# A graph layer on one core: the own side computed from 128 nodes in fp32, and nine batches of rows fetched row by row by ScalarE and SyncE instead of three by ScalarE

## The chip, the core and the metric

The kernel runs on one core of a Trainium2 chip. The metric is the device time of one launch in microseconds: before the change 3934.06 us, median of three runs (3931.01 to 3935.81).

## What is computed

```python
theta = x[dst] - x[src]                       # 412,500 edges, 128 features, fp32
w = sigmoid(relu(theta @ W1 + b1) @ W2 + b2)
agg = segment_sum(w * theta, dst)             # 12,500 nodes; the edges are sorted by dst
indeg = segment_sum(1, dst)
out = layernorm(x + agg + indeg * (x @ W4 + b4))
```

Since theta @ W1 is x[dst] @ W1 - x[src] @ W1, the kernel first projects every node (u = x @ W1) and keeps u and x side by side in a table in HBM, 256 fp32 values (1 KB) a node. For each edge it then needs the row of its source (u for the weight, x for the sum), which is random, and the projection of its destination, the *own side*, which is near in number for neighbouring edges.

## The kernel before, in words

**Tiling.** The edges are cut into 112 chunks of at most 28 tiles of 128 edges; a chunk touches at most 128 neighbouring destination nodes, its window. A chunk is four batches of seven tiles (896 edges), called j = 0 to 3; with a short tail batch there are 449, numbered g.

**Where the rows of the sources come from.** 425 batches are *ringed*: GpSimd gathers them with one indirect DMA a tile (`windows_gpsimd`, L783), into six slots in turn; it may start batch n once batch n-6 has been scaled (`scaled`) and the own side of batch n-2 is there (`z_ready`). 21 batches are *held*: their x rows were gathered at the start (L768), and PE projects them in steps between the other batches. Three batches are fetched *by hand*: ScalarE loads the seven source numbers of one row of tiles into registers (L891) and issues seven DMAs of 1 KB, one for each tile (L895), 128 rows for a batch, one row with each batch g from 40 on. All three share one buffer, since nearly all of the held rows are still in use when it is filled.

**The own side.** x of the window arrives transposed (`winT`) and PE multiplies it with W1 and W4 (`project_window`, L820); DVE adds the biases (`take_window`, L1038 and L1040), which gives `own`, the projections of the window's 128 nodes, and `lin`. `own` in fp32 is then split into three bf16 numbers for each value: ScalarE rounds it (`high`, L910), DVE takes the rest (`take_high`, L1044), ScalarE rounds that (`mid`, L914), DVE takes the last part (`low`, L1048). SyncE stores the three parts to HBM (L672) and loads, for each batch, the 126 rows of 42 nodes from which that batch's own side comes (L666), since a batch touches at most 42 nodes. PE then multiplies these 126 rows with a one-hot matrix in bf16 (L794), whose column for an edge has three ones.

**The rest of a batch.** ScalarE makes the one-hot matrix in two steps (`distance` L875, `one_hot` L883), three batches ahead. DVE subtracts the gathered u (L998), applies relu and the weights W2 (L1004), makes the other one-hot matrix (L1017) and sums to logits (L1012); ScalarE takes the sigmoid (`gate`, L902 and L904); DVE scales x (L1027); PE adds the batch up by node (`add_up`, L812, fp32). In batch j = 1 of a chunk DVE takes the sums of the chunk before (L1033) and finishes its rows (L1060 to L1068), and in j = 2 it normalises them (L971 to L1076).

**Order.** Each engine works through a list written out by hand, in order. SyncE's loop (`windows_sync`) does this for chunk c: `store_parts(c + 1)`, in the middle of which the window of chunk c + 2 is loaded (`load_window`, L690 and L691, after `rows_done`), and then `store_result(c - 1)` (L699), which waits for the normalised rows, that is until batch j = 2 of chunk c. PE's `project_window(c + 2)` stands in chunk c at j = 2 and DVE's `take_window(c + 2)` in chunk c at j = 3.

Of the kernel before, what the change touches and what calls it, by code (L numbers as in the profile page):

```python
# [4 lines left out]
FP32 = mybir.dt.float32  # L5
# [6 lines left out]
P = 128  # L12
# [4 lines left out]
ROUND = 12582912.0  # L17

# [8 lines left out]
NEAR = 42  # L27
WK = 3 * NEAR
# [6 lines left out]
SLOTS = 4  # L35
# [9 lines left out]
HAND = 3  # L45
HAND_FROM = 40
EARLY = 3
# [22 lines left out]
class Sizes:  # L70

    def __init__(self, nodes, edges):
# [28 lines left out]
        self.hand = [HAND_FROM + (P + 2) * (m + 1) + m for m in range(HAND)]  # L101
        assert self.hand[-1] < self.batches and HAND_FROM > self.held[1] and not set(self.hand) & set(self.held)
# [28 lines left out]
def build(nc, x, src, dst, W1, b1, W2, b2, W4, b4, x_cols, x_turned, held_src, src_rows, dst_rows_in, firsts, out):  # L131
    z = Sizes(x.shape[0], src.shape[0])
    with ExitStack() as ctx:
# [15 lines left out]
        near_of = nc.dram_tensor("near_of", (z.rows, NB), FP32, kind="Internal").ap()  # L149
        parts_of = nc.dram_tensor("parts_of", (SLOTS, 3 * P, F), BF16, kind="Internal").ap()  # L150

# [11 lines left out]
        part_no = sb("part_no", [P, 1])  # L163
        node_no = sb("node_no", [P, 1])
# [6 lines left out]
        near_all = sb("near_all", [P, z.rows * NB])  # L171
        near_row = sb("near_row", [P, z.rows * NB], I32)
        neg_ids = sb("neg_ids", [P, z.rows * NB])
# [12 lines left out]
        near_lin = sb("near_lin", [P, NB])  # L186
        last_lin = sb("last_lin", [P, NB])
        held_ends = sb("held_ends", [P, 2])
        none = sb("none", [P, P], I32)
        beyond = sb("beyond", [P, 3, P], I32)  # L190
        extremes = sb("extremes", [P, 10])
        loop_gaps = sb("loop_gaps", [P, PIECES])
        wrong = sb("wrong", [P, 12])
# [8 lines left out]
        parts = sb("parts", [P, 2 * NB, F], BF16)  # L202
        away = sb("away", [P, 2, BATCH], BF16)
        hot_ne = sb("hot_ne", [P, 2, BATCH], BF16)
# [9 lines left out]
        own = sb("own", [P, F])  # L214
        rest = sb("rest", [P, F])
        stage = sb("stage", [P, 2, 3, F], BF16)
# [39 lines left out]
        hand_x = slots_of_x[:, 0:2 * BT * F].rearrange("p (t f) -> p t f", f=2 * F)  # L256
# [57 lines left out]
        const_chain = sem("const_chain")  # L314
# [8 lines left out]
        near_lin_ready = sem("near_lin_ready")  # L323
        near_of_out = sem("near_of_out")
        near_in = sem("near_in")
        near_ready = sem("near_ready")
# [19 lines left out]
        high_ready = sem("high_ready")  # L346
        rest_ready = sem("rest_ready")
        mid_ready = sem("mid_ready")
        low_ready = sem("low_ready")
        parts_out = sems("parts_out", 2)  # L350
        parts_in = sems("parts_in", 2 * NB)
# [67 lines left out]
        def near_no(g):  # L419
            r, j = row_and_place(g)  # L420
            return r * NB + j

# [25 lines left out]
        def hand_row(g):  # L448
            for m, at in enumerate(z.hand):
                row = g - (z.hand[m - 1] + 2 if m else HAND_FROM)  # L450
                if g < at:
                    return (m, row) if 0 <= row < P else None
            return None
# [32 lines left out]
        def place_rows(dve):  # L486
# [20 lines left out]
            for n in range(PIECES):  # L507
# [21 lines left out]
            v.tensor_scalar(held_ends[held_rows, :], row_dst[held_rows, 0:2 * (BATCH - 1):BATCH - 1],  # L529
                            row_base[held_rows, :], None, ALU.subtract)  # L530
# [7 lines left out]
            for bit in range(BITS):  # L538
# [9 lines left out]
            firsts_of = work[0:R, 0:CHUNK].rearrange("p (j e) -> p j e", e=BATCH)  # L548
            v.tensor_scalar(last_lin[0:R, 0:NB - 1], firsts_of[:, 0:NB - 1, BATCH - 1], row_gap[0:R, :], None, ALU.add)
            link(v.tensor_scalar(near_lin[0:R, :], firsts_of[:, :, 0], row_gap[0:R, :], 0.0, ALU.add, ALU.max))  # L550
            link(v.tensor_scalar(near_lin[0:R, :], near_lin[0:R, :], float(P - NEAR), None, ALU.min))
            v.tensor_copy(last_lin[held_rows, 0:1], held_ends[held_rows, 1:2])
            v.tensor_scalar(near_lin[held_rows, 0:1], held_ends[held_rows, 0:1], 0.0, float(P - NEAR), ALU.max, ALU.min)\
                .then_inc(near_lin_ready, 1)
            dve.wait_ge(near_lin_ready, 1)

            for n, at in enumerate((0, P, CHUNK - P)):
                v.tensor_scalar(end_at[0:R, n:n + 1], row_end[0:R, :], float(at), None, ALU.subtract)
            link(v.tensor_copy(last_lin[0:R, NB - 1:NB], extremes[0:R, 5:6]))
# [24 lines left out]

        def place_near(dve):
            v = nc.vector
            dve.wait_ge(near_in, 16)
            v.tensor_scalar(near_row[:, :], near_all[:, :], 3.0, None, ALU.mult).then_inc(near_ready, 1)
            v.tensor_scalar(neg_ids[:, :], near_all[:, :], node_no[:, :], -1.0, ALU.add, ALU.mult)\
                .then_inc(near_ready, 1)  # L590

# [72 lines left out]
        def load_parts(sp, g, row):  # L664
            buf = g % (2 * NB)
            sp.dma_start(parts[0:WK, buf, :], parts_of[chunk_of(g) % SLOTS, bass.ds(row, WK), :])\  # L666
                .then_inc(parts_in[buf], 16)

        def store_parts(sp, c):
            sp.wait_ge(low_ready, c + 1)  # L670
            sp.sem_inc(sp_gate, 1)
            sp.dma_start(parts_of[c % SLOTS, :, :].rearrange("(p m) f -> p m f", m=3), stage[:, c % 2, :, :])\  # L672
                .then_inc(parts_out[c % 2], 16)
            if 0 < c < last_chunk:
                wait(sp, rows_done, c - 1)
                sp.wait_ge(win_ready, c)
                sp.sem_inc(sp_gate, 1)
                load_window(sp, c + 1)
            sp.wait_ge(parts_out[c % 2], 16 * (c // 2 + 1))
            sp.sem_inc(sp_gate, 1)  # L680
            lo, hi = c * NB, end_of(c)
            rows = clamped(near_row, near_no(lo), near_no(lo) + NB, 3 * (P - NEAR))
            if c == last_chunk:
                rows = rows + clamped(near_row, near_no(z.batches), near_no(z.batches) + 1, 3 * (P - NEAR))
            for g in range(lo, hi):
                load_parts(sp, g, rows[g - lo])

# [5 lines left out]
        def store_result(sp, c):  # L693
            sp.wait_ge(y_ready, c + 1)
            if c:
                sp.wait_ge(y_out[(c - 1) % 2], 16 * ((c - 1) // 2 + 1))
            sp.sem_inc(sp_gate, 1)
            base = clamped(base_i, c, c + 1, z.last_base)[0]
            sp.dma_start(out[bass.ds(base, P), :], yout[:, c % 2, :]).then_inc(y_out[c % 2], 16)  # L699

        def windows_sync(sp):
# [22 lines left out]
            for k in range(z.groups):  # L724
# [5 lines left out]
            sp.wait_ge(near_lin_ready, 1)  # L730
            sp.sem_inc(sp_gate, 1)
            sp.dma_start(near_of, near_lin[0:z.rows, :]).then_inc(near_of_out, 16)
            sp.wait_ge(near_of_out, 16)
            sp.sem_inc(sp_gate, 1)
            sp.dma_start(near_all[:, :], near_of.rearrange("(a r) j -> a (r j)", a=1).to_broadcast([P, z.rows * NB]))\
                .then_inc(near_in, 16)
# [680 lines left out]
```

## Time and profile before

| | |
|---|---|
| time, median of 3 runs | 3934.06 us |
| profiled execution: its own time, its span | 3929.44 us, 3927.6 us |
| DVE busy, POOL busy | 2979.7 us (76%), 2953.8 us (75%) |
| PE busy, weight loads | 2018.4 us (51%), 1781.0 us (45%) |
| ScalarE busy | 1255.4 us (32%) |
| mean granted TensorE clock | 0.619 |
| DMA engines | 147 GB/s, about half busy |

Busy shares leave out what an engine's sequencer does by itself: register loads, waits and the issue of DMAs. SyncE does nothing else and so has no busy time at all, and part of ScalarE's list is of this kind. "issue" in a chain or a wait is time in which an engine waited for nothing that the profile shows.

### The profile page before, as it was taken

The page shows a single profiled execution, that of the slowest core. Times are in us where ns is not written, and L with a number is a line of the kernel's source. Part 1 is how long each engine was busy: PE and PEld are TensorE (multiplying, and loading weights), DVE is VectorE, ACT ScalarE, POOL GpSimd, SP SyncE. Part 2 cuts the span into 40 slices and gives each one's busy share as a digit, 9 for nine tenths or more (in the row PEclk, how much of TensorE's full clock was granted, in tenths as well). Part 3 has the DMA queues.
Part 4 walks back from the last instruction along what each step waited for, and adds up shares of the span by engine and source line. Part 5 has one row for each costly group of instructions (what it writes and reads, how often), then busy time and mean ns, then how long its engine had stood idle before and what let it go on. Part 6 is the DMA issues. An engine that isn't in the chain of part 4 may idle for free.

```text
span 3927.6 us, 48444 instructions
## 1 busy us (share of the span) xinstructions
PE 2018.4 (51%) x10531; PEld 1781.0 (45%) x10531; DVE 2979.7 (76%) x4855; ACT 1255.4 (32%) x2220; POOL 2953.8 (75%) x3123
## 2 busy tenths in 40 slices
PE   3245555555545555555555555555555555555554
PEld 2244444444444444444444444444444444444444
DVE  7568777777777777777777777778778777777777
ACT  1223333333333333333333333333333333333332
POOL 7777777777777777777777777777777777777776
PEclk5565665566666556665666656666666665665666
DMA  7445455555555555555555545555555555555553
GB/s 234 131 138 148 144 147 143 146 147 147 147 147 147 147 147 148 146 148 147 147 147 143 148 145 147 147 146 148 148 146 147 147 148 145 146 148 144 149 147 105
DMA packets 343028, 577.99 MB, mean 147 GB/s; under 512 B 127642, under 2 KB 216768, under 8 KB 342501
## 3 DMA queue, kind: packets, MB, share of 16 engines
q0 software_dynamic: 147264, 399.12, 36.0%
q10 hardware_dynamic: 49501, 110.40, 8.7%
q1 hardware_dynamic: 145970, 65.36, 6.2%
q8 instruction: 87, 1.43, 0.1%
q14 instruction: 206, 1.69, 0.1%
HBM read 549.00 MB, written 31.99 MB: 148 GB/s over the span
## 4 chain that ended last, share of the span: by engine, by line
POOL 60%; issue 24%; DVE 8%; ACTq 4%; ACT 2%; DMA 1%; PE 0%; POOLq 0%; DVEq 0%
POOL arena L783 56%; POOL held_x L768 4%; ACTq L895 3%; DVE logit L1012 2%; DVE diff L1004 2%; DVE ps_both L998 1%; DMA arena<-table,lists 1%; ACT away L875 1%; ACTq L891 1%; DVE edge_rows L1027 1%; DVE edge_rows L1017 1%; ACT hot_ne L883 0%; ACT ps_log L902 0%; DVE square L976 0%; DVE rstd L978 0%
## 5 line engine op out<-in xcount | busy, mean ns | idle before, releaser
L783 POOL DMA_INDIRECT arena<-table,lists x2970 | 2810.2, 946 | 905.0 <-issue 899.5
L875 ACT ACTIVATE away<-dst_rows,neg_ids 126x896 bf16<-126x896 bf16 (+1 forms) x449 | 466.4, 1039 | 1587.6 <-issue 1587.6
L812 PE MATMUL ps_win<-edge_rows 128*128 128x130 f32 x3140 | 716.3, 416 | 424.7 <-DVE edge_rows L1027 406.7
L812 PE MATMUL ps_sum<-edge_rows 128*128 128x130 f32 x3136 | 713.4, 415 | 422.2 <-DVE edge_rows L1027 404.3
L812 PEld LDWEIGHTS ps_win<-edge_rows 128*128 128x128 f32 x3140 | 663.2, 319 | 482.8 <-issue 482.6
L812 PEld LDWEIGHTS ps_sum<-edge_rows 128*128 128x128 f32 x3136 | 660.1, 318 | 480.2 <-issue 479.6
L998 DVE TENSOR_TENSOR ps_both<-ps_both,arena 128x896 f32<-128x896 f32 x425 | 467.0, 1099 | 485.6 <-DMA arena<-table,lists 482.0
L794 PE MATMUL ps_both<-parts,hot_ne 126*128 126x128 bf16 x3138 | 334.3, 266 | 958.7 <-ACT hot_ne L883 633.7
L794 PEld LDWEIGHTS ps_both<-parts,hot_ne 126*128 126x128 bf16 x3138 | 245.9, 118 | 1072.1 <-issue 569.7
L1027 DVE TENSOR_TENSOR edge_rows<-arena,ps_log 128x896 f32<-128x896 f32 x425 | 461.5, 1086 | 129.2 <-ACT ps_log L902 129.0
L1004 DVE SCALAR_TENSOR_TENSOR diff<-ps_both,w_rows 128x896 f32<-128x896 f32 (+1 forms) x449 | 489.4, 1090 | 15.4
L1017 DVE TENSOR_TENSOR edge_rows<-ps_log,lists 128x896 f32<-128x896 f32 (+1 forms) x449 | 484.8, 1080 | 0.0
L1012 DVE TENSOR_REDUCE logit<-diff 128x7 f32<-128x896 f32 (+1 forms) x449 | 482.3, 1074 | 0.0
L883 ACT ACTIVATE hot_ne<-away,ones_col 126x896 bf16<-126x896 bf16 (+1 forms) x449 | 467.1, 1040 | 43.2 <-ACT away L875 1.5
L902 ACT ACTIVATE ps_log<-logit,b_col 128x7 f32<-128x7 f32 (+1 forms) x449 | 120.4, 268 | 900.1 <-DVE logit L1012 899.6
L768 POOL DMA_INDIRECT held_x<-in_x,held_at x147 | 143.1, 973 | 50.0 <-issue 47.6
L1048 DVE TENSOR_TENSOR stage<-rest,stage 128x128 bf16<-128x128 f32 x112 | 32.8, 292 | 167.2 <-ACT stage L914 166.8
L904 ACT ACTIVATE edge_rows<-logit,b_col 128x7 f32<-128x7 f32 (+1 forms) x449 | 130.8, 291 | 0.1
L976 DVE SCALAR_TENSOR_TENSOR square<-rstd,neg_half 128x1 f32<-128x1 f32 x336 | 74.5, 222 | 12.0
L644 PE MATMUL ps_hid<-w,held_xT 128*128 128x128 f32 x294 | 71.4, 383 | 0.0
L644 PEld LDWEIGHTS ps_hid<-w,held_xT 128*128 128x128 f32 x294 | 66.5, 306 | 0.0
L978 DVE SCALAR_TENSOR_TENSOR rstd<-square,rstd 128x1 f32<-128x1 f32 x336 | 54.1, 161 | 11.5
(136 smaller groups left out, 1198.6 us busy)
## 6 DMA issues: line engine op xcount, KB each, us to landing
dst_rows<-rel_of ACTq DMA_DIRECT2D x224, 441.0 KB
arena<-table,lists POOLq DMA_INDIRECT x2970
held_x<-table ACTq DMA_DIRECT2D x2688, 1.0 KB
parts<-parts_of SPq DMA_DIRECT2D x449, 31.5 KB
parts_of<-stage SPq DMA_DIRECT2D x112, 96.0 KB, 3.4
winT<-in_x_cols SPq DMA_DIRECT2D x112, 64.0 KB
window<-in_x SPq DMA_DIRECT2D x112, 64.0 KB
out<-yout SPq DMA_DIRECT2D x112, 64.0 KB
```

Source lines behind the costliest of these rows:

```text
L644: last = nc.tensor.matmul(ps_hid[:, (2 + t) * P:(3 + t) * P], held_xT[:, t, :], w14[:, 0:F], start=True, stop=True)
L768: nc.gpsimd.indirect_dma_start(held_x[:, h * BT + t, :], None, x, ids).then_inc(held_in, 16)
L783: nc.gpsimd.indirect_dma_start(gath[:, slot_of(g) + t, :], None, table, ids)\
L794: last = nc.tensor.matmul(ps_z[b][:, t, :], hot_ne[0:WK, b, t * P:(t + 1) * P], parts[0:WK, buf, :], start=True, stop=True)
L812: last = nc.tensor.matmul(ps_sums(c), hot_en[:, b, t, :], scaled_x[:, b, t, :], start=(j == 0 and t == 0), stop=(stop and t == tiles_of(g) ...
L875: nc.scalar.activation(away[0:WK, b, 0:n], dst_rows[0:WK, p % 2, lo:lo + n], ACT.Abs, bias=neg_ids[0:WK, near_no(g):near_no(g) + 1]).then_ ...
L883: nc.scalar.activation(hot_ne[0:WK, b, 0:n], away[0:WK, b, 0:n], ACT.Relu, bias=ones_col[0:WK, :], scale=-1.0).then_inc(hot_ready, 1)
L998: v.tensor_tensor(ps_z[b][:, 0:n, :], ps_z[b][:, 0:n, :], u, ALU.subtract).then_inc(z_read, 1)
L1004: v.scalar_tensor_tensor(diff[:, 0:n, :], ps_z[b][:, 0:n, :], 0.0, w2_rows[:, :].rearrange("p (a f) -> p a f", a=1).to_broadcast([P, n, F] ...
L1012: v.tensor_reduce(logit[:, b, 0:n], diff[:, 0:n, :], AX.X, ALU.add).then_inc(logit_ready, 1)
L1017: v.tensor_tensor(hot_en[:, b, 0:n, :], ps_col.rearrange("p (a n) -> p a n", a=1).to_broadcast([P, n, P]), rel[:, lo:lo + n].rearrange("p ...
L1027: v.tensor_tensor(scaled_x[:, g % SB, 0:n, 0:F], rows, ps_wgt(g).rearrange("p (t a) -> p t a", a=1).to_broadcast([P, n, F]), ALU.mult)\
```

## The change

Four things are changed.

1. *Own side.* The split into three parts is gone, with `high`, `mid`, `take_high`, `low`, `store_parts`, `load_parts` and the small tables for them. `own` has two buffers. PE multiplies the fp32 one-hot matrix (now 128 rows) with all 128 rows of `own`, in fp32.
2. *Hand-fetched batches.* There are nine instead of three, one for every 43 batches, in two buffers in turn. Of the 128 rows of each, ScalarE fetches the last 43, one with each batch g from 40 on as before, and SyncE the first 85. GpSimd gathers 419 batches instead of 425.
3. *SyncE's list.* For chunk c it now loads the window of chunk c + 1, fetches two rows, stores the result of chunk c - 1, and fetches six rows (from chunk 10 on; 765 rows in all).
4. *Windows.* `project_window(c + 2)` stands at j = 3 of chunk c instead of j = 2, and `take_window(c + 2)` at j = 0 of chunk c + 1 instead of j = 3 of chunk c.

```diff
-HAND = 3
+HAND = 9
 HAND_FROM = 40
+SPAN = 43
+SP_ROWS = P - SPAN
+SP_FROM = HAND_FROM // NB
+SP_EACH = (2, 6)
...
+        def sync_rows(c):
+            lo = (c - SP_FROM) * sum(SP_EACH)
+            return [divmod(n, SP_ROWS) for n in range(lo, lo + sum(SP_EACH)) if 0 <= n < HAND * SP_ROWS]
+
+        def hand_free(m):
+            return (z.hand[m - 2] if m >= 2 else z.held[2 * m + 1]) + 1
+
+        def hand_transfers(eng, kind, m, row):
+            lo = first_tile(z.hand[m])
+            ids = nc.values_load_multi_w_load_instructions(
+                src_at[row:row + 1, lo:lo + BT], engines=[kind], min_val=0, max_val=z.nodes - 1,
+                skip_runtime_bounds_check_because="src holds numbers of nodes")[1]
+            for t in range(BT):
+                eng.dma_start(hand_x[row:row + 1, m % 2, t, :], table[bass.ds(ids[t], 1), :])\
+                    .then_inc(hand_in[2 * m + t % 2], 16)
...
+        def fetch_hand_row(sp, m, row):
+            if row == 0:
+                sp.wait_ge(scaled, hand_free(m))
+                sp.sem_inc(sp_gate, 1)
+            hand_transfers(sp, mybir.EngineType.SP, m, row)
...
-            store_parts(sp, 0)
-
             for c in range(last_chunk + 1):
-                if c < last_chunk:
-                    store_parts(sp, c + 1)
+                if 0 < c < last_chunk:
+                    wait(sp, rows_done, c - 1)
+                    sp.wait_ge(win_ready, c)
+                    sp.sem_inc(sp_gate, 1)
+                    load_window(sp, c + 1)
+                rows = sync_rows(c)
+                for m, row in rows[:SP_EACH[0]]:
+                    fetch_hand_row(sp, m, row)
                 if c:
                     store_result(sp, c - 1)
+                for m, row in rows[SP_EACH[0]:]:
+                    fetch_hand_row(sp, m, row)
             store_result(sp, last_chunk)
...
                 for t in range(tiles_of(g)):
-                    last = nc.tensor.matmul(ps_z[b][:, t, :], hot_ne[0:WK, b, t * P:(t + 1) * P],
-                                            parts[0:WK, buf, :], start=True, stop=True)
+                    last = nc.tensor.matmul(ps_z[b][:, t, :], hot_ne[:, b, t * P:(t + 1) * P], own[:, c % 2, :],
+                                            start=True, stop=True)
                 last.then_inc(z_ready, 1)
...
-                if j == 2 and c + 2 <= last_chunk:
+                if j == 3 and c + 2 <= last_chunk:
                     project_window(c + 2)
...
-                if j == 1 and c < last_chunk:
-                    low(c + 1)
                 one_hot_rows(g)
                 add_logit(g)
                 if g == 0:
                     take_window(1)
-                if j == 3 and c + 2 <= last_chunk:
-                    take_window(c + 2)
+                if j == 0 and 0 < c < last_chunk:
+                    take_window(c + 1)
...
-                if j == 0 and c < last_chunk:
-                    take_high(c + 1)
```

SyncE's list from the storing of one result to the loading of the next window, in the middle of the kernel, before. `base_i` holds the windows' first nodes, `near_row` the places of the batches' parts.

```order
L660 TENSOR_LOAD base_i [waits y_ready,y_out1]
L699 ISA
L699 DMA out<-yout 128x128
L672 DMA parts_of<-stage 128x384 [waits low_ready]
L660 TENSOR_LOAD base_i [waits rows_done,win_ready]
L690 REGISTER_ALU
L690 DMA winT<-in_x_cols 128x128
L691 ISA
L691 DMA window<-in_x 128x128
```

The same place now (chunk 10). `lists` holds the source numbers, and `held_x` is the memory in which the hand-fetched rows are put.

```order
L622 TENSOR_LOAD base_i [waits y_ready,y_out0]
L637 ISA
L637 DMA out<-yout 128x128
L431 TENSOR_LOAD lists
L435 ISA
L435 DMA held_x<-table 1x256
...
L622 TENSOR_LOAD base_i [waits rows_done,win_ready]
L628 REGISTER_ALU
L628 DMA winT<-in_x_cols 128x128
L629 ISA
L629 DMA window<-in_x 128x128
```

Where "..." stands, the last three rows go on until six register loads and 42 one-row DMAs have been issued. Between the result that is stored and the next window stood one DMA before; now these six rows stand there.

DVE around `take_window`, before: it stands in j = 3, behind that batch's logits.

```order
L1012 TENSOR_REDUCE logit<-diff 128x7 [waits relu_ready,wgt_col_ready]
L1038 TENSOR_TENSOR own<-ps_sum,b_rows 128x128 [waits low_ready,win_ready]
L1040 TENSOR_TENSOR lin<-ps_sum,b_rows 128x128 [waits rows_done]
L1027 TENSOR_TENSOR edge_rows<-arena,ps_log 128x7x128 [waits wgt_ready]
L998 TENSOR_TENSOR ps_both<-ps_both,arena 128x896 [waits gathered2,z_ready]
```

And now, one batch later (j = 0 of the next chunk), with the batch j = 1 behind it, in which the sums of the chunk before are taken:

```order
L929 TENSOR_REDUCE logit<-diff 128x7 [waits relu_ready,wgt_col_ready]
L954 TENSOR_TENSOR own<-ps_sum,b_rows 128x128 [waits win_ready]
L956 TENSOR_TENSOR lin<-ps_sum,b_rows 128x128 [waits rows_done]
L944 TENSOR_TENSOR edge_rows<-arena,ps_log 128x7x128 [waits wgt_ready]
L915 TENSOR_TENSOR ps_both<-ps_both,arena 128x896 [waits gathered3,z_ready]
L921 SCALAR_TENSOR_TENSOR diff<-ps_both,w_rows 128x896 [waits logit_ready,z_read]
L934 TENSOR_TENSOR edge_rows<-ps_log,lists 128x896 [waits summed]
L929 TENSOR_REDUCE logit<-diff 128x7 [waits relu_ready,wgt_col_ready]
L950 COPY sums<-ps_win 128x130 [waits summed]
L944 TENSOR_TENSOR edge_rows<-arena,ps_log 128x7x128 [waits wgt_ready]
```

`win_ready` is raised by PE's `project_window`, which waits for both window DMAs of SyncE. The wait for it has moved one batch later, and everything behind it on DVE's list still stands behind it.

## Rows read from the trace of the kernel before

**Rows 1.** The page, chain of work that ended last: shares by line.
```profile
POOL arena L783 56%; POOL held_x L768 4%; ACTq L895 3%; DVE logit L1012 2%; DVE diff L1004 2%; DVE ps_both L998 1%; DMA arena<-table,lists 1%; ACT away L875 1%; ACTq L891 1%; DVE edge_rows L1027 1%; DVE edge_rows L1017 1%; ACT hot_ne L883 0%; ACT ps_log L902 0%; DVE square L976 0%; DVE rstd L978 0%
```
**Rows 2.** The page, costliest groups: busy us, mean ns | idle before, releaser.
```profile
L783 POOL DMA_INDIRECT arena<-table,lists x2970 | 2810.2, 946 | 905.0 <-issue 899.5
```
**Rows 3.** All waits: us in total, times, longest us.
```profile
POOL arena L783 <- DVE edge_rows L1027: 3.4, 11, 0.3
```
**Rows 4.** SyncE's queue after one normalised result, chunks 10, 105 and 106.
```profile
563.84 0.39 SPq L699 DMA_DIRECT2D out<-yout  x1
...
3708.71 0.39 SPq L699 DMA_DIRECT2D out<-yout  x1
...
3742.66 0.39 SPq L699 DMA_DIRECT2D out<-yout  x1
```
**Rows 5.** SyncE's register load of four numbers: ns, least, median and most.
```profile
L660 SPq TENSOR_LOAD <-near_row x113: 274/304/505, 160.1 to 3861.9; - x113
```
**Rows 6.** ScalarE's load of seven numbers and its one-row DMAs, by line.
```profile
L891 ACTq TENSOR_LOAD <-lists x384: 1131/1736/1815, 542.0 to 3774.6; - x192
...
L895 ACTq DMA_DIRECT2D held_x<-table x2688: 231/235/480, 543.9 to 3778.5; - x192
```
**Rows 7.** SyncE's second window DMA, by line.
```profile
L691 SPq DMA_DIRECT2D window<-in_x x112: 333/345/1393, 12.6 to 3831.2; - x112
```
**Rows 8.** Timeline, all engines, one chunk: start us, us, what, idle before.
```profile
2605.35 1.04 ACT L875 ACTIVATE away<-dst_rows,neg_ids 126x896 bf16<-126x896 bf16 x1 [4.41 <-issue]
...
2610.70 1.09 DVE L1027 TENSOR_TENSOR edge_rows<-arena,ps_log 128x896 f32<-128x896 f32 x1 [0.20 <-ACT ps_log L902]
...
2611.70 0.38 DVE L1060 TENSOR_SCALAR plus_one<-sums 128x2 f32<-128x2 f32 x1
...
2613.40 0.35 SPq L690 DMA_DIRECT2D winT<-in_x_cols  x1
2613.55 1.10 DVE L998 TENSOR_TENSOR ps_both<-ps_both,arena 128x896 f32<-128x896 f32 x1
...
2613.95 0.34 SPq L691 DMA_DIRECT2D window<-in_x  x1
...
2614.91 1.96 SPq L666 DMA_DIRECT2D parts<-parts_of  x4
...
2616.69 1.08 DVE L1012 TENSOR_REDUCE logit<-diff 128x7 f32<-128x896 f32 x1
...
2618.16 1.09 DVE L1027 TENSOR_TENSOR edge_rows<-arena,ps_log 128x896 f32<-128x896 f32 x1 [0.40 <-ACT ps_log L902]
...
2618.59 1.17 PE L820 MATMUL ps_win<-w,winT 128*128 128x256 f32 x2
...
2619.85 2.81 ACTq L895 DMA_DIRECT2D held_x<-table  x7
...
2621.24 0.35 DVE L1076 SCALAR_TENSOR_TENSOR yout<-y,mv,rstd 128x128 f32<-128x128 f32 x1
...
2622.32 0.39 SPq L699 DMA_DIRECT2D out<-yout  x1
...
2625.09 0.91 PE L794 MATMUL ps_both<-parts,hot_ne 126*128 126x128 bf16 x7 [2.91 <-ACT hot_ne L883]
2625.84 0.28 DVE L1038 TENSOR_TENSOR own<-ps_win,b_rows 128x128 f32<-128x128 f32 x1
...
2626.31 1.09 DVE L1027 TENSOR_TENSOR edge_rows<-arena,ps_log 128x896 f32<-128x896 f32 x1
```
**Rows 9.** DMA issues: KB each, median us from issue to landing.
```profile
parts_of<-stage SPq DMA_DIRECT2D x112, 96.0 KB, 3.4
...
w<-in_L_gnn_W SPq DMA_DIRECT2D x2, 64.0 KB, 2.6
```
**Rows 10.** Timeline: one batch added up by PE in fp32.
```profile
2611.89 3.37 PE L812 MATMUL ps_sum<-edge_rows 128*128 128x130 f32 x14 [3.31 <-DVE edge_rows L1027]
```
**Rows 11.** The queue's own waits: SyncE, us in total, times, longest us.
```profile
SPq L671 <- DVE stage L1048: 2111.1, 112, 55.1
```

More of the change, by code:

```diff
@@ L34 @@
 SB = 3
-SLOTS = 4
 DB = 2
@@ L100, in __init__ @@
         self.held = [c * NB for c in self.held_chunks]
-        self.hand = [HAND_FROM + (P + 2) * (m + 1) + m for m in range(HAND)]
-        assert self.hand[-1] < self.batches and HAND_FROM > self.held[1] and not set(self.hand) & set(self.held)
+        self.hand = [HAND_FROM + SPAN * (m + 1) + 2 * NB for m in range(HAND)]
+        assert self.hand[-1] < self.batches and not set(self.hand) & set(self.held)
+        assert HAND_FROM > self.held[1] and HAND_FROM + SPAN > self.held[3] and sum(SP_EACH) * SPAN >= SP_ROWS * NB
         assert min(b - a for a, b in zip([0] + self.held, self.held)) >= PAIRS * STEPS and self.groups > 16
@@ L213, in build @@
         lin = sb("lin", [P, 3, F])
-        own = sb("own", [P, F])
-        rest = sb("rest", [P, F])
-        stage = sb("stage", [P, 2, 3, F], BF16)
+        own = sb("own", [P, 2, F])
         carry_sel = sb("carry_sel", [P, 2, P])
@@ L448, in hand_row @@
         def hand_row(g):
[L449 to L453, printed above, removed]
+            m, row = divmod(g - HAND_FROM, SPAN)
+            return (m, SP_ROWS + row) if 0 <= m < HAND else None
+        def sync_rows(c):
[11 more added lines that the diff above has]
+                    .then_inc(hand_in[2 * m + t % 2], 16)
         def held_step(g):
@@ L547, in place_rows @@
             link(v.tensor_scalar(work[0:R, 0:CHUNK], loops_out[0:R, 0:CHUNK], NONE, None, ALU.bitwise_and))
[L548 to L555, printed above, removed]
             for n, at in enumerate((0, P, CHUNK - P)):
-                v.tensor_scalar(end_at[0:R, n:n + 1], row_end[0:R, :], float(at), None, ALU.subtract)
-            link(v.tensor_copy(last_lin[0:R, NB - 1:NB], extremes[0:R, 5:6]))
+                last = v.tensor_scalar(end_at[0:R, n:n + 1], row_end[0:R, :], float(at), None, ALU.subtract)
+            link(last)
             for n in range(3):
@@ L662, in clamped @@
                 skip_runtime_bounds_check_because="place_bases clamps it to this range")[1]
[L664 to L686, printed above, removed]
         def load_window(sp, c):
@@ L882, in one_hot @@
                 act.wait_ge(away_ready, g + 1)
-                nc.scalar.activation(hot_ne[0:WK, b, 0:n], away[0:WK, b, 0:n], ACT.Relu, bias=ones_col[0:WK, :],
+                nc.scalar.activation(hot_ne[:, b, 0:n], away[:, b, 0:n], ACT.Relu, bias=ones_col[:, :],
                                      scale=-1.0).then_inc(hot_ready, 1)
             def fetch_hand(m, row):
-                if row == 0:
-                    act.wait_ge(scaled, (z.hand[m - 1] if m else z.held[1]) + 1)
+                if row == SP_ROWS:
+                    act.wait_ge(scaled, hand_free(m))
                     act.sem_inc(act_gate, 1)
-                lo = first_tile(z.hand[m])
-                ids = nc.values_load_multi_w_load_instructions(
-                    src_at[row:row + 1, lo:lo + BT], engines=[mybir.EngineType.Activation], min_val=0,
-                    max_val=z.nodes - 1, skip_runtime_bounds_check_because="src holds numbers of nodes")[1]
-                for t in range(BT):
-                    nc.scalar.dma_start(hand_x[row:row + 1, t, :], table[bass.ds(ids[t], 1), :])\
-                        .then_inc(hand_in[2 * m + t % 2], 16)
+                hand_transfers(nc.scalar, mybir.EngineType.Activation, m, row)
             def gate(g):
@@ L905, in gate @@
                     .then_inc(wgt_col_ready, 1)
-            def high(c):
-                act.wait_ge(own_ready, c + 1)
-                wait(act, parts_out[c % 2], 16 * (c // 2))
-                nc.scalar.copy(stage[:, c % 2, 0, :], own[:, :]).then_inc(high_ready, 1)
-            def mid(c):
-                act.wait_ge(rest_ready, c + 1)
-                nc.scalar.copy(stage[:, c % 2, 1, :], rest[:, :]).then_inc(mid_ready, 1)
             for k in range(z.groups):
@@ L1023, in scale_rows @@
                 b, n = g % 2, tiles_of(g)
-                rows = hand_x[:, :, F:2 * F] if g in hand_no else held_x[:, held_no[g] * BT:held_no[g] * BT + n, :] if g in held_no else \
+                rows = hand_x[:, hand_no[g] % 2, :, F:2 * F] if g in hand_no else held_x[:, held_no[g] * BT:held_no[g] * BT + n, :] if g in held_no else \
                     gath[:, slot_of(g):slot_of(g) + n, F:2 * F]
```

113 lines of the change are left out of this document (21 added, 92 removed).

## The prediction
> **What bounds the kernel now.** I read the chain of waits first: 56% of the span is the gathers on POOL [rows 1], and most of the rest is issue time. The groups say what that is: 2970 gathers of 946 ns, with 905.0 us of idle time between them that is all issue, 0.305 us each [rows 2]. So a gather takes 1.251 us from start to start, a batch of seven 8.76, and 2970 of them 3715 us of a span of 3927.6. The list of waits says that POOL hardly ever waits for anybody: 3.4 us for DVE's scaling, 11 times [rows 3]. POOL is the bound, from 194 us on, and each batch taken from it is worth 8.76 us as long as everyone else keeps up. Then I looked at how regular the chunks are. SyncE stores one result a chunk; between chunk 10 (563.84) and chunk 105 (3708.71) lie 95 chunks of 33.10 us [rows 4]. Last I read SyncE's own list, since the change puts work there: it mostly stands still, 2111.1 us in front of the part that DVE makes last [rows 11]. The timeline of one chunk gives the distances that I add up below [rows 8].
>
> **What goes, and what it is worth.** Six batches leave POOL: 42 gathers at 1.251 us, 52.5 us. The split of the own side goes (four small operations and a wait for ScalarE a chunk); it stands beside POOL's work and is worth nothing by itself, but gives DVE some slack. Storing and loading the parts leaves SyncE.
>
> **The own side on PE.** Seven fp32 products of 128 rows take about what `add_up` takes, 3.37 us [rows 10], where the bf16 ones took about 0.9. PE then has 2 x 3.37 a batch, 27.0 a chunk, 1.17 for the window and some 2 for held rows and the carry: 30 us in 33.1. It is prepared two batches ahead of DVE, so I cost it at nothing; uncovered it would be 2.5 us a batch. ScalarE's two steps keep their 896 columns; two more rows cost nothing. ScalarE's fetching keeps its pace, one row a batch.
>
> **What one row costs SyncE.** This is the term that decides. A row is one load of seven numbers and seven DMAs. SyncE's load of four numbers took 304 ns, 505 at most [rows 5], and from the end of its DMA at 2614.29 to the next one behind such a load passed 0.62 us [rows 8]. Seven one-row DMAs in a row take ScalarE 2.81 us, 0.235 each and the rest between them [rows 6, 8]. That makes 3.43. The same DMA on SyncE can be held up when ScalarE issues too (L691: 345 ns median, 1393 most) [rows 7], so I take r = 3.55 us. Bounds: from below 0.30 + 7 x 0.235 = 1.95 with nothing between them; from above what a row costs ScalarE, 4.41 us of its list [rows 8], or with its load of 1.74 as well as the gaps some 4.9 [rows 6]. I stay near 3.5, since SyncE's own load and its own gap are in the rows.
>
> The Trainium skill, "DMA: Bandwidth & Descriptors", section "Latency and other measured facts", gives about 600 ns as the floor of a register load. SyncE's 304 ns stands below that floor, so I go by the row; by the page r would be about 3.85 and the time some 170 us longer.
>
> Eight rows are 28.4 us a chunk, the window and the result about 3 more: 31.5 in 33.1. By the sum alone it fits. It is the order that does not.
>
> **Where the wait lies.** Follow one chunk c. DVE ends `yout` in j = 2; call this T. SyncE stores the result, then issues six rows, and only then the window of chunk c + 2. PE wants that window in j = 3 of the same chunk, DVE wants its projection behind the logits of the next batch, about T + 13 us at today's pace. Six rows alone are 21.3 us. So DVE stops at `take_window`, and only after it comes the work that leads to the next `yout`. That makes a loop through SyncE, PE and DVE, once a chunk:
>
> - from the end of `yout` (2621.59) to the end of the store's DMA (2622.71): 1.12 [rows 8]
> - six rows: 21.3
> - the load of the window's first node and what lies around it 0.62, from the first window DMA to the second 0.55 [rows 8], landing 2.6, as for the 64 KB of W [rows 9]: 3.77
> - PE's projection, 1.17 and its start: 1.3
> - DVE from `own` to the end of that batch's scaling, 2625.84 to 2627.40: about 1.5
> - batch j = 1: to the end of the logits 4.22 (2613.55 to 2617.77), 0.39 for the sigmoid, 1.0 for the scaling, 1.85 for finishing the rows (2611.70 to 2613.55): 7.45
> - batch j = 2 to the end of `yout`, 2613.55 to 2621.59: 8.04 [rows 8]
>
> Sum 23.2 + 6r = 44.5 us. Beside it PE adds up the batch j = 3 (3.37), which `take_sums` in j = 1 needs, and makes the own side for j = 2 (3.37): 6.7 behind the window, while DVE comes to them after 9. ScalarE needs 4.41 and two steps of 1.04 between two sigmoids, 7.4, and DVE takes as long. SyncE's other two rows fall under DVE's 17 us. The next loop starts at 44.5, not at 33.1, and POOL, six slots and two own sides ahead at most, stands and waits.
>
> **The sum.** Up to chunk 10 nothing changes: 563.8. Then 95 chunks of 44.5: 4228. Chunk 105 has three rows behind its result: 23.2 + 10.7 = 34. The last stretch took 3927.6 - 3742.7 = 185 and now POOL is ahead, 175. Span 5001, with the 1.84 us that lie around it 5003; the profiled execution (3929.4) stands 4.7 below the median. I say **5000 us**, 27% slower. The gain of 52.5 is not in it, since POOL no longer binds.
>
> **The rivals.**
>
> *A. SyncE's rows are cheaper than ScalarE's.* For it: ScalarE's load takes 1.74 us where SyncE's takes 0.30. Against it: the DMAs are the larger part, and SyncE's four part loads stand 0.54 apart, wider than ScalarE's. With r = 2.4 the loop is 37.6 and the time 563.8 + 3572 + 30 + 175 = 4340; slower still. The loop equals today's 33.1 at r = 1.65, under my lower bound.
>
> *B. The window comes in time and POOL stays the bound: faster.* Then the six batches come back in full, 3929.4 - 52.5 = 3877. This would need SyncE to issue the window before those rows, or r below about 1.5. For it: SyncE stands still over half of the time, and the sum of its new work is less than a chunk. Against it: the order, in which the window stands behind the six rows with no way around.
>
> The Trainium skill, the same page, section "Issuing engines are not separate DMA queues", says that issuing from several engines saves only the sequencer's time to start a DMA, "usually small relative to the DMA itself". By this rule the rows would cost little wherever they stand, which is B's 3877. The trace does not agree here: 49 register and DMA instructions for six rows are 21 us in which nothing else on SyncE's list can start.
>
> *C. A row costs SyncE as much as ScalarE or more,* because both issue small DMAs at once. r = 4.4 gives a loop of 49.6 and 563.8 + 4712 + 36 + 175 = 5490. For it: the 1393 ns of rows 7. Against it: more than half of those issues kept their 0.34.
>
> *D. PE is the bound.* 30 us a chunk is under 33.1, so this alone would take back none of the 52.5; with a loop of 44.5 PE has room. If the own side at j = 2 came later by 5 us, each loop would be 3 us longer, 5280. That the change doesn't do what it says I give no chance: the list shows the rows on SyncE.
>
> **Chances.** My forecast, r between 3.0 and 4.1, loops of 41.2 to 47.8 and times of 4690 to 5320: 0.74. A with r under 3.0: 0.12. C and D beyond 5320: 0.08. B, or another way below 3926: 0.05. No change: 0.01; the range is from 4600 to 5330. Less than 0.2%, 8 us, can't be told from no change for this kernel. Slower 0.94, same 0.01, faster 0.05.
>
> **What would show it.** Results stored by SyncE about 44.5 us apart between chunks 10 and 105, and about 33 before. DVE waiting at `own` for PE some 10 us a chunk, PE's projection for the window DMA, and POOL for `z_ready` or `scaled`, which it never did. On SyncE, from the store to the first window DMA about 22 us, seven DMAs and a load at 3.5 us. POOL's gathers still 1.25 us apart where it runs. It is wrong if the results stay 33 us apart (B), or if the time between them is not 23 + 6r with the r that the trace shows.

## The result, and the profile after

The changed kernel takes **5544.06 us** (median of four runs, 5542.76 to 5546.28) against 3934.36 for the kernel before: 1.409 times as long, 95% interval 1.408 to 1.411. Slower, as forecast, but 544 us above the 5000 that I named and outside the range of 4600 to 5330. In three later groups of runs every kernel, the one before included (4731 to 4778 us), ran a fifth longer than elsewhere; no time of those groups is set beside a time from outside it, and the readings below rest on the groups in which the kernel before took 3930 to 3934 us.

The chain of waits (page of the changed kernel, shares by engine and by line) has gone from POOL [rows 1] to SyncE's queue. `SPq` is that queue; L435 are the one-row DMAs and L431 the register loads.

```profile
SPq 42%; DVE 22%; issue 19%; POOL 8%; DMA 4%; PE 3%; ACT 1%; ACTq 1%; DVEq 0%; POOLq 0%
SPq L435 22%; SPq L431 17%; POOL arena L724 5%; DVE diff L921 4%; DVE ps_both L915 4%; DVE logit L929 4%; DVE edge_rows L944 4%; DMA window<-in_x 3%; POOL held_x L709 3%; SPq L622 2%; DVE square L893 1%; PE ps_sum L761 1%; PE ps_win L761 1%; ACT ps_log L837 1%; DVE rstd L895 1%
```

The gathers' group on the same page answers to [rows 2]. One gather still takes 946 ns, but POOL now stands still for 2559 us, of which 1711 wait for PE's own side.

```profile
L724 POOL DMA_INDIRECT arena<-table,lists x2928 | 2770.9, 946 | 2559.3 <-PE ps_both L735 1710.9
```

Why PE is late the list of waits says (us in total, times, longest): PE waits for the window's DMA, and DVE for PE's projection of it, 2239 us in 96 waits.

```profile
PE ps_win L761 <- DMA window<-in_x: 1263.4, 49, 28.2
PE ps_sum L761 <- DMA window<-in_x: 1259.6, 50, 28.4
DVE own L954 <- PE ps_win L761: 1123.1, 48, 24.9
DVE own L954 <- PE ps_sum L761: 1115.9, 48, 24.9
```

96 is the number of chunks whose windows stand behind rows of SyncE. So DVE stands 23.3 us a chunk at `own`, where I had named some 10. Its work in a loop is 24.9 us (990.93 us busy in the 2000 us from 600 on, times 50.16), so nearly all of its idle time now stands at this one place; before the change it was idle 7.7 us of 33.10 as well (1535.68 busy in the same stretch), and the 10 left that out.

SyncE's queue over one loop (timeline: start, us, what; x42 are six rows, x14 two) shows the order at work:

```profile
563.87 0.38 SPq L637 DMA_DIRECT2D out<-yout  x1
...
615.52 0.39 SPq L637 DMA_DIRECT2D out<-yout  x1
617.67 26.77 SPq L435 DMA_DIRECT2D held_x<-table  x42
645.36 0.36 SPq L628 DMA_DIRECT2D winT<-in_x_cols  x1
645.92 0.36 SPq L629 DMA_DIRECT2D window<-in_x  x1
648.01 7.50 SPq L435 DMA_DIRECT2D held_x<-table  x14
666.81 0.38 SPq L637 DMA_DIRECT2D out<-yout  x1
```

Up to chunk 10 nothing has changed: the result that SyncE stores in it goes out at 563.87, where it was 563.84 [rows 4]. The loop from 615.52 on takes 51.3 us. Of it 29.5 lie between the end of the store and the next window DMA; an estimated 0.63 for the window's own load (I had 0.62) leaves 28.8 for six rows, 4.80 a row. The rest of the loop is 22.5. Between chunks 10 and 105 the results are (5328.62 - 563.87) / 95 = 50.16 us apart, where they were 33.10.

What makes a row so long are the loads (all instructions of the line: ns, least, median and most, by engine; first the loads, then the DMAs):

```profile
L431 SPq TENSOR_LOAD <-lists x765: 928/1732/1984, 533.7 to 5338.9; - x192
L431 ACTq TENSOR_LOAD <-lists x387: 1132/1753/1814, 541.9 to 5363.7; - x194
```

```profile
L435 SPq DMA_DIRECT2D held_x<-table x5355: 224/228/462, 535.4 to 5343.3; - x199
```

A load of seven source numbers takes SyncE 1.73 us, what it takes ScalarE [rows 6], and not what a load of four of another table took SyncE [rows 5]. The DMAs cost what I took.

### The profile page after: what moved, and what is told of

Same layout as the page of the kernel before. It is cut to its first block, busy times and chain, and to the rows that moved or that the text cites. A ratio compares the mean times of both kernels' runs of the same rounds, so it can differ in the third digit from the quotient of the medians.

```text
span 5542.7 us, 69098 instructions
## 1 busy us (share of the span) xinstructions
PE 2141.8 (39%) x13669; PEld 2031.1 (37%) x13669; DVE 2908.9 (52%) x4615; ACT 1216.2 (22%) x1996; POOL 2914.4 (53%) x3081
## 4 chain that ended last, share of the span: by engine, by line
SPq 42%; DVE 22%; issue 19%; POOL 8%; DMA 4%; PE 3%; ACT 1%; ACTq 1%; DVEq 0%; POOLq 0%
SPq L435 22%; SPq L431 17%; POOL arena L724 5%; DVE diff L921 4%; DVE ps_both L915 4%; DVE logit L929 4%; DVE edge_rows L944 4%; DMA window<-in_x 3%; POOL held_x L709 3%; SPq L622 2%; DVE square L893 1%; PE ps_sum L761 1%; PE ps_win L761 1%; ACT ps_log L837 1%; DVE rstd L895 1%
## 5 line engine op out<-in xcount | busy, mean ns | idle before, releaser
L735 PE MATMUL ps_both<-own,hot_ne 128*128 128x128 f32 x6276 | 994.3, 322 | 701.6 <-ACT hot_ne L824 518.3
L735 PEld LDWEIGHTS ps_both<-own,hot_ne 128*128 128x128 f32 x6276 | 926.0, 233 | 748.7 <-issue 468.5
L816 ACT ACTIVATE away<-dst_rows,minus_row 128x896 bf16<-128x896 bf16 (+1 forms) x449 | 466.2, 1038 | 1587.0 <-issue 1587.0
L761 PE MATMUL ps_win<-w,winT 128*128 128x256 f32 x114 | 66.4, 685 | 1263.4 <-DMA window<-in_x 1263.4
L761 PE MATMUL ps_sum<-w,winT 128*128 128x256 f32 x110 | 64.5, 688 | 1259.6 <-DMA window<-in_x 1259.6
L753 PE MATMUL ps_win<-edge_rows 128*128 128x130 f32 x3140 | 491.6, 320 | 40.4 <-DVE edge_rows L944 38.5
L753 PE MATMUL ps_sum<-edge_rows 128*128 128x130 f32 x3136 | 491.2, 320 | 30.3 <-DVE edge_rows L944 27.4
L753 PEld LDWEIGHTS ps_win<-edge_rows 128*128 128x128 f32 x3140 | 480.9, 236 | 55.7 <-issue 46.2
L753 PEld LDWEIGHTS ps_sum<-edge_rows 128*128 128x128 f32 x3136 | 480.9, 237 | 46.5 <-issue 37.2
L824 ACT ACTIVATE hot_ne<-away,ones_col 128x896 f32<-128x896 bf16 (+1 forms) x449 | 467.0, 1040 | 42.7 <-ACT away L816 1.1
```

The source lines that it names most:

```text
L735: last = nc.tensor.matmul(ps_z[b][:, t, :], hot_ne[:, b, t * P:(t + 1) * P], own[:, c % 2, :], start=True, stop=True)
L753: last = nc.tensor.matmul(ps_sums(c), hot_en[:, b, t, :], scaled_x[:, b, t, :], start=(j == 0 and t == 0), stop=(stop and t == tiles_of(g) ...
L816: nc.scalar.activation(away[:, b, 0:n], dst_rows[:, p % 2, lo:lo + n], ACT.Abs, bias=minus_row[:, :]).then_inc(away_ready, 1)
L824: nc.scalar.activation(hot_ne[:, b, 0:n], away[:, b, 0:n], ACT.Relu, bias=ones_col[:, :], scale=-1.0).then_inc(hot_ready, 1)
```

## The experiments

**Own side alone.** Is any of the loss in the fp32 own side or in the later windows?

```diff
-HAND = 9
+HAND = 3
...
-        self.hand = [HAND_FROM + SPAN * (m + 1) + 2 * NB for m in range(HAND)]
+        self.hand = [HAND_FROM + (P + 2) * (m + 1) + m for m in range(HAND)]
...
-                rows = sync_rows(c)
+                rows = []
```

The lines left out give ScalarE all 128 rows of the three batches again.

> Part 1 and part 4 of the change alone: own side in fp32 from 128 nodes, windows projected and taken one batch later, three hand-fetched batches by ScalarE on the old places, nothing fetched by SyncE. Theory (the loop through SyncE makes the whole loss): POOL stays the bound with 2970 gathers, 3930 us, within 0.2% of before. Rival (the fp32 own side makes PE late): each chunk longer than 33.1 us, 3950 us or more, and POOL waiting for z_ready.

3930.63 us against 3930.38: ratio 1.0001 (0.9991 to 1.0011). No loss and no gain. POOL's gathers are as before (2970, with 900 us of issue between them); all their other waits are 5 us together.

**No rows by SyncE.** What is the gain if POOL keeps binding?

```diff
-                rows = sync_rows(c)
+                rows = []
...
-                        dve.wait_ge(hand_in[2 * hand_no[g] + q], 16 * P * len(range(q, BT, 2)))
+                        dve.wait_ge(hand_in[2 * hand_no[g] + q], 16 * SPAN * len(range(q, BT, 2)))
```

> As the changed kernel, but SyncE fetches none of its 765 rows (rows 0 to 84 of the nine hand batches hold old numbers, so that part of the sums is left out); 419 ringed batches on POOL. Theory: without the rows the loop is 23.2 us and POOL binds, 3934 - 52.5 = 3882 us, 1.3% faster than before. Rival (something else in the change costs the time): the time stays above 4000 us.

3876.95 us, ratio 0.9864 (0.9847 to 0.9880): 53.4 us less in the median, where 42 gathers were costed at 52.5. So the whole loss comes with the 765 rows that SyncE fetches; ScalarE's share of all nine batches is in this kernel and costs nothing.

**The window first.** Is it the order or the amount?

```diff
-            for c in range(last_chunk + 1):
+            def next_window(c):
                 if 0 < c < last_chunk:
                     wait(sp, rows_done, c - 1)
...
                     load_window(sp, c + 1)
+
+            next_window(1)
+            for c in range(last_chunk + 1):
                 rows = sync_rows(c)
                 for m, row in rows[:SP_EACH[0]]:
                     fetch_hand_row(sp, m, row)
                 if c:
                     store_result(sp, c - 1)
+                    next_window(c + 1)
                 for m, row in rows[SP_EACH[0]:]:
                     fetch_hand_row(sp, m, row)
```

> As the changed kernel, but SyncE loads the next window directly behind the stored result, ahead of the six rows instead of behind them. Same work, other order. Theory (order): the loop 23.2 + 6r is gone; what is left is SyncE's own sum, eight rows of 4.75 us and some 3 us for window and result, 41 us a chunk: 564 + 95 x 41 + 34 + 180 = 4670 us. Rival (only the amount on SyncE or the DMA traffic counts): the time stays near 5540 us. Second rival (the sum of SyncE's work is hidden): 3880 us.

4529.95 us, ratio 1.1524 (1.1504 to 1.1543). Only the place of two DMAs a chunk is another, and 1014 us of the 1610 are gone. In a second group, beside the changed kernel:

> The window directly behind the stored result, loads as in the changed kernel. 4530 us as before where the kernel before takes 3930 (40.6 us a chunk, SyncE's own sum); 0.82 of after_again.

4531.35 us against 5543.41 for the changed kernel run again, 0.817:

> The changed kernel itself, as the mark for the other three in this job. Theory: 1.41 times the kernel before where that takes 3930 us (5544). Where the kernel before takes 4730, all that SyncE issues is slower too, and it takes 6700 or more.

The queue of SyncE in window_first_b, from one stored result to the next:

```profile
2631.85 0.39 SPq L637 DMA_DIRECT2D out<-yout  x1
2632.82 0.36 SPq L628 DMA_DIRECT2D winT<-in_x_cols  x1
2633.38 0.36 SPq L629 DMA_DIRECT2D window<-in_x  x1
2635.66 36.09 SPq L435 DMA_DIRECT2D held_x<-table  x56
2672.50 0.39 SPq L637 DMA_DIRECT2D out<-yout  x1
```

SyncE never stands still here: 40.65 us for eight rows, a window and a result. The forecast for it was 41 a chunk; the time came out 140 us below 4670 mainly because not all chunks need that: between chunks 10 and 105 the median is 40.6, but 20 of the 95 take 36.0 to 36.7, where the loads are the short ones (below).

**Fewer numbers in a load.** Only the term that I now held to be too small is changed: the same 5355 DMAs behind shorter loads, four numbers from column 256 on.

```diff
+            if kind == mybir.EngineType.SP:
+                lo = 256
+            n = 4 if kind == mybir.EngineType.SP else BT
...
-                src_at[row:row + 1, lo:lo + BT], engines=[kind], ...
+                src_at[row:row + 1, lo:lo + n], engines=[kind], ...
...
-                eng.dma_start(hand_x[row:row + 1, m % 2, t, :], table[bass.ds(ids[t], 1), :])\
+                eng.dma_start(hand_x[row:row + 1, m % 2, t, :], table[bass.ds(ids[t % n], 1), :])\
```

> The changed kernel with SyncE's load of four numbers from a multiple of four on, three of them used twice. Theory (the load is the mis-sized term): a row 3.3 us, the loop 43 us, 4860 us, that is 0.88 of after_again. Rival (SyncE's and ScalarE's one-row DMAs hold each other up): within 3% of after_again.

4789.86 us, 0.864 of the changed kernel in the same group, where 4860 and 0.88 were forecast. SyncE's loads and its queue over one loop:

```profile
L434 SPq TENSOR_LOAD <-lists x765: 298/562/787, 534.8 to 4584.4; - x192
```

```profile
2633.28 0.38 SPq L640 DMA_DIRECT2D out<-yout  x1
2634.18 18.94 SPq L438 DMA_DIRECT2D held_x<-table  x42
2653.87 0.36 SPq L631 DMA_DIRECT2D winT<-in_x_cols  x1
2654.44 0.36 SPq L632 DMA_DIRECT2D window<-in_x  x1
...
2675.21 0.38 SPq L640 DMA_DIRECT2D out<-yout  x1
```

A row now takes (2653.87 - 0.63 - 2633.66) / 6 = 3.26 us and the loop 41.9, that is 22.4 + 6 x 3.26. With ScalarE issuing beside it as before, the rival of rows that hold each other up is out.

The median of 0.56 hides two values for one and the same load. Here are two loads of SyncE from this loop, the first right behind the stored result, the second behind the seven one-row DMAs of a row:

```profile
L434 SPq TENSOR_LOAD <-lists x1: 311/311/311, 2633.7 to 2633.7; - x1
L434 SPq TENSOR_LOAD <-lists x1: 588/588/588, 2636.7 to 2636.7; - x1
```

Over the whole run the 192 loads that stand behind a stored result or a window's DMA have a median of 0.31 us, the 573 behind a row's DMAs 0.57. The load that I had taken my price from [rows 5] stands behind a window's DMA [rows 8].

**Four rows before the result and four behind it.**

```diff
-SP_EACH = (2, 6)
+SP_EACH = (4, 4)
```

> The kernel of rows_4_4 where the kernel before takes 3930 us: the changed kernel with four rows ahead of the stored result and four behind. Theory: the larger of 22.4 + 4 x 4.74 = 41.4 and SyncE's sum 40.6, so 41.4 us a chunk, 4640 us (5544 less 96 times 9.4). Rival (eight rows stand in the way wherever they are): 5540.

4685.15 us, ratio 1.1916 (1.1892 to 1.1940), 1% above the 4640 named. Same rows, same DMAs, two rows moved by one place: 859 us less than the changed kernel. SyncE's queue:

```profile
3040.40 0.39 SPq L637 DMA_DIRECT2D out<-yout  x1
3042.58 17.34 SPq L435 DMA_DIRECT2D held_x<-table  x28
3060.68 0.36 SPq L628 DMA_DIRECT2D winT<-in_x_cols  x1
3061.25 0.35 SPq L629 DMA_DIRECT2D window<-in_x  x1
3063.38 16.77 SPq L435 DMA_DIRECT2D held_x<-table  x28
3082.30 0.38 SPq L637 DMA_DIRECT2D out<-yout  x1
```

(3060.05 - 3040.79) / 4 = 4.8 a row and a loop of 41.9: 22.7 + 4 x 4.8. Three loops with other numbers or lengths of rows thus give the same rest, 22.5, 22.4 and 22.7 us (as medians over all such loops 22.2, 22.4 and 22.5).

**What a load costs.** The first probe put one more load on SyncE in each chunk of the kernel before:

> The kernel before, with one more register load on SyncE in each chunk, its result unused: for nine chunks each one of twelve kinds that differ in how many numbers are loaded (1, 2, 4, 7, 8), at which offset from a multiple of four (0 to 3) and from which partition (0 or 50). The changed kernel's loads of seven took 1.2 us for the two batches whose numbers begin at a multiple of four and 1.75 for the others, the load of four before 0.30. Theory (how many numbers, and how they lie): seven at offset 0 take 1.2 us and at the other offsets 1.75, four at offset 0 take 0.3 on either partition, eight at offset 0 take 0.3 to 0.6. Rival (the partition): all loads from partition 0 take 0.3 to 0.5, those from 50 more. Time of the kernel 3930 us, as SyncE has room.

Nothing used the numbers, and the loads were left out of the program; 3931.42 us says nothing on them. The next gave each number a DMA:

```diff
...
+                if 24 < c <= 32 and c <= last_chunk:
+                    ids = sp_probe(src_at[0:1, 256:260], **kw)[1]
...
+                for t in range(len(ids)):
+                    sp.dma_start(probe_out[8 * c + t:8 * c + t + 1, :], table[bass.ds(ids[t], 1), :]).then_inc(probe_sem, 16)
```

This is one of the 14 kinds.

> The kernel before, with one more register load on SyncE in each chunk behind the stored result, and one one-row DMA for each number loaded (from the table to an unused place in HBM). In the probe before it the loads were left out of the program, since nothing used their numbers. Fourteen kinds, eight chunks each: 1, 2, 3, 4, 5, 7 or 8 numbers, beginning 0 to 3 numbers behind a multiple of four, on partition 0 or 50. Theory (how many numbers, and how they lie): from partition 0 seven at offset 0 take 1.2 us and at the other offsets up to 1.75, four at offset 0 take 0.3, four at offset 1 over 1; partition 50 the same. Rival (the partition or the tile): all loads from partition 0 take 0.3 to 0.5, those from 50 more. The DMAs take 0.23 us each. Time of the kernel 3931 us.

It ran twice, in groups where the kernel before took 4778 and 4732 us, with single loads from 0.00 to 1.6 us. Medians of the second, eight loads a kind: four numbers from a multiple of four 0.70 (partition 0) and 0.34 (partition 50), eight 0.52, seven from a multiple of four 0.96 and 0.98, seven from one number behind it 1.48 and 0.98. In the first run partition 50 came out the slower one for four numbers (0.50 against 0.30) and for the last kind (1.53 against 1.25). So the probe settles nothing by itself, and the answer comes from the runs outside these groups. Medians of SyncE's loads that stand behind a row's DMAs: four numbers from a multiple of four 0.57, eight 0.80 (below), seven from a multiple of four 1.21 (the changed kernel's fourth and eighth batch, in the queue between 2196 and 2640 six rows in 23.8 instead of 26.7 us), seven from elsewhere 1.77. Eight numbers cost less than seven. The rival of the partition falls there too: in the second batch of four_numbers_c such loads stay at 0.55 to 0.62 from partition 2 to 84, all but one.

**Both repaired.** Window first, and eight numbers from a multiple of four on:

```diff
-        self.hand = [HAND_FROM + SPAN * (m + 1) + 2 * NB for m in range(HAND)]
+        self.hand = [next(g for g in range(HAND_FROM + SPAN * (m + 1) + 2 * NB, self.batches)
+                          if g % NB in (0, NB - 1) and g not in self.held) for m in range(HAND)]
...
+            skip = lo % 4
...
-                src_at[row:row + 1, lo:lo + BT], engines=[kind], ...
+                src_at[row:row + 1, lo - skip:lo - skip + 8], engines=[kind], ...
...
-                eng.dma_start(hand_x[row:row + 1, m % 2, t, :], table[bass.ds(ids[t], 1), :])\
+                eng.dma_start(hand_x[row:row + 1, m % 2, t, :], table[bass.ds(ids[skip + t], 1), :])\
```

The hand-fetched batches now stand only at j = 0 or 3, where `skip` is 0 or 1. `next_window` is that of the window first.

> The window directly behind the stored result and loads of eight numbers from a multiple of four on. Theory: a row 3.5 us, SyncE 31 us a chunk, POOL binds, 3880 us. Rival (the load keeps its 1.75): as window_first_b. Second rival (a row of 3.8): 3950.

3904.83 us, ratio 0.9931 (0.9914 to 0.9947): 0.7% faster than before, between the theory and the second rival.

```profile
L434 SPq TENSOR_LOAD <-lists x765: 527/799/984, 535.4 to 3711.5; - x192
```

```profile
2614.63 0.39 SPq L640 DMA_DIRECT2D out<-yout  x1
...
2617.43 29.57 SPq L438 DMA_DIRECT2D held_x<-table  x56
2647.76 0.39 SPq L640 DMA_DIRECT2D out<-yout  x1
```

SyncE needs 33.1 us a chunk (a load took 0.80, not 0.5), a little more than POOL's 32.55, (3144.9 - 52.5) / 95. So I took one row a chunk from it:

```diff
-HAND = 9
-SPAN = 43
-SP_EACH = (2, 6)
+HAND = 8
+SPAN = 47
+SP_EACH = (2, 5)
```

> The version of eight_aligned_c with eight hand batches instead of nine, one for every 47: SyncE fetches seven rows a chunk (81 of each batch), ScalarE one with each batch (47). In eight_aligned_c SyncE's sum was 33.0 us a chunk, just over POOL's 32.6, and the time 3905 us. Theory: with seven rows SyncE needs 29.2 us, POOL binds and keeps the whole gain of 35 gathers, 35 x 1.251 = 43.8 us: 3888 us, 1.1% faster than before. Rival (something besides SyncE's sum held nine back): 3900 us or more.

**3887.94 us**, ratio 0.9888 (0.9871 to 0.9904), the 3888 forecast; it beats both kernels. SyncE waits for DVE's result again, 82 times, and POOL for nobody:

```profile
SPq L638 <- DVE yout L990: 990.1, 82, 115.2
```

```profile
POOL arena L731 <- issue: 889.1, 2915, 0.3
```

**The same kernels beside a kernel before of 4731 to 4778 us.** Three of the kernels above had first run in those groups (kernel before in the group in brackets): eight_aligned 5989.80 and, again, 6002.75 (4732, 4731); four_numbers 6261.40 and 6339.80 (4778, 4732); rows_4_4 6531.10 and 6493.65 (4778, 4732). The expectations for two of them:

> As the changed kernel, but SyncE loads for each of its rows only four numbers, from a multiple of four on, and uses three of them twice: the same 5355 DMAs, other rows fetched, so that part of the sums is of other rows. Theory (the load is the term that was too small, 1.75 us instead of 0.30 in six rows a loop): a row takes 3.3 us, the loop 23.2 + 6 x 3.3 = 43.0, the time 564 + 95 x 43.0 + 33 + 178 = 4860 us. Rival (the one-row DMAs on SyncE and ScalarE hold each other up): the time stays above 5300.

> As the changed kernel, but SyncE fetches four rows ahead of the stored result and four behind it instead of two and six. Same work. Theory (loop 22.4 + 4.74 x rows behind the result, or SyncE's sum of 40.6, the larger): 22.4 + 19.0 = 41.4 us a chunk, 564 + 95 x 41.4 + 41 + 178 = 4716 us. Rival (eight rows stand in the way wherever they are): 5540.

All six times lie far above their forecasts. There the ratio of eight_aligned is 1.27 and not 0.99, so this isn't one factor for all kernels. A gather kept its length (0.949 us), but SyncE's 56 one-row DMAs took 54 us in eight_aligned instead of 29.6. The cause stays open: no run separates the chip from what is loaded or issued.

## Why the prediction was wrong

*POOL is the bound, 1.251 us a gather, 52.5 us for 42.* Right: no_sync_rows kept 53.4 of them, eight_batches 43.9 for 35 gathers (43.8 costed).

*The own side costs nothing, nor does its split.* Right, to 0.1% (own_only).

*The wait stands at the window, behind six rows, and makes a loop through SyncE, PE and DVE.* Right, and shown by three changes of it: the window ahead of the rows (1014 us less), four rows behind the result instead of six (859 less), cheaper rows (754 less). POOL waits for the own side, as named.

*The loop without its rows, 23.2 us.* 22.4 to 22.7 in the kernels tried; the seven terms together were 0.5 to 0.8 too large.

*The first ten chunks, 563.8, and the last stretch, 175.* 563.87, and 5542.7 - 5367.94 = 174.8.

*A row costs SyncE 3.55 us.* **This step failed.** It is 4.80, and 4.2 in the 20 of the 95 loops where the load is the short one. I took the load from SyncE's load of four numbers of `near_row`, 0.62 with what lies around it [rows 5, 8], for seven numbers of `lists`, and dismissed ScalarE's 1.74 [rows 6] as ScalarE's own. What was measured: SyncE's load of these numbers takes 1.73, as ScalarE's did. It hangs on how many numbers there are, on where they begin and on what stands in front of the load, and hardly on the engine. Two gaps add up to the error: the same load of four costs 0.57 behind a row's DMAs and 0.31 behind a window's, where I had read it, and behind a row's DMAs seven numbers from elsewhere cost 1.77 where four cost 0.57. From store to first row passed 1.76 us where I had 0.62; the DMAs were right (0.228 for 0.235). The load is off by 1.43 at the median, against which the 0.12 that I had added for issues that hold each other up was not needed. The other loops took 50.9 us in the mean and the 20 with short loads 47.1 to 47.8. Over all 95 the results were 50.16 - 44.5 = 5.66 us further apart than forecast, 538 us, and chunk 105 with its three rows took 39.3 for 34. That is the 544, but for 1.

The row for it was in my hands: a load of seven numbers from the same tile [rows 6]. The reason I gave for staying near 3.5, that SyncE's own load was in the rows, compared the engine and forgot the operand. My upper bound, 4.4 to 4.9, held the truth; the range was cut at r = 4.1.

*Rivals.* A (cheaper rows) and B (hidden) are out, B's 3877 being what the kernel would give without SyncE's rows. C named the size, 5490, for a reason that was wrong: four_numbers_c shows the DMAs of both engines side by side at 3.26 a row. D is out: PE has room even in a chunk of 33 us (own_only).

*What I drew from the pages.* The Trainium skill, "DMA: Bandwidth & Descriptors", section "Issuing engines are not separate DMA queues", calls the time to start a DMA "usually small relative to the DMA itself". That compares one start with one DMA, and no row here shows how long a one-row DMA takes to land. What the runs contradict is what I made of it, B's 3877: the starts and loads of eight rows take 36 us of SyncE's 40.65 in window_first_b, and they are the bound there. (Six rows are 48 loads and DMAs; the 49 in the prediction is one too many.) The Trainium skill, same page, section "Latency and other measured facts", gives about 600 ns as the floor of a register load. Here it is no floor, since four numbers load in 0.30 to 0.31 us [rows 5], and for seven numbers it lies far under the 1.73.

## What to carry to other kernels

Work put on an idle queue costs by what stands behind it in the list, not by its share of the queue: draw the loop from the wait it delays to the wait that feeds it, and put the transfer that others wait for ahead of the filler. A duration is taken from a row with the same operand and shape, and with the same instructions in front of it, before one with the same engine. Then compare the queue's own sum with the bound's pace: here nine batches with eight rows a chunk on SyncE gained 26.7 us, eight batches with seven rows 43.9.

## What the runs showed of the hardware

*Register loads.* Eight numbers from a multiple of four on load in a median of 0.80 us on SyncE and 0.74 on ScalarE (eight_aligned_c), seven in 1.73 and 1.75 (the changed kernel, with its two batches of shorter loads counted in). On SyncE a load right behind the DMA of a window or a result is cheaper by about a quarter of a microsecond than the same load behind a row's seven DMAs: 0.31 against 0.57 for four numbers, 0.55 against 0.80 for eight, 1.56 against 1.77 for seven from elsewhere. No run shows why.

*The granted clock.* Between 2600 and 3400 us TensorE's mean granted clock was 0.62 before and 0.82 in own_only, with 2922 matmul instructions in the stretch where there were 2239. Its two levels are 1.2 and 2.4 GHz, and a mean of 1.00 is the higher one. First before, then own_only:

```profile
2600.00:3400.00 800.00, 426.74 (x2239) 376.17 (x2240) 620.62 (x1023) 267.54 (x478) 605.29 (x640) 0.62 0.51 147
2600.00:3400.00 800.00, 484.91 (x2922) 446.95 (x2921) 608.42 (x974) 258.40 (x429) 604.92 (x641) 0.82 0.47 141
```

(Columns: stretch, us, PE, PEld, DVE, ACT and POOL busy with counts, clock, DMA share, GB/s.) So the own side in fp32 took PE to 485 us instead of 427. One batch of it, costed at 3.37 us, took 3.30 in a stretch mostly at the lower level and 1.80 at the higher one (own_only, the own side's instructions alone; columns: stretch, us, PE, PEld, clock, DMA share, GB/s):

```profile
2607.00:2611.00 4.00, 3.30 (x14) 3.04 (x14) 0.58 0.73 220
2616.00:2618.00 2.00, 1.80 (x14) 1.63 (x14) 1.00 0.38 117
```

In the changed kernel, where PE waits for windows, the mean was 0.67 in the same 800 us.
